# A transformer layer on one core: heads visited three score tiles at a time, sums in groups of 384 and 128 queries, and stacks loaded 16 rows at a time

## The chip, the cores and the metric

The kernel runs on one core of a Trainium2 chip. The metric is the device time of one execution in microseconds (us). PE is TensorE, DVE is VectorE, ACT is ScalarE, POOL is GpSimd and SP is SyncE, which here only issues DMAs and waits.

## The reference

One layer on 4 sequences of 2048 tokens, width 256: layer norm, then attention with 16 heads of 16 channels and a learned bias by relative position, plus a feed-forward branch scaled by a router's gate, plus the residual. The change is in the attention:

```python
    q, k, v = (qkv[:, :, 0], qkv[:, :, 1], qkv[:, :, 2])
    scores = jnp.einsum('bhqd,bhkd->bhqk', q, k)
    scores = scores + compute_bias(rel_emb, S, S)
    attn = jax.nn.softmax(scores.astype(jnp.float32), axis=-1).astype(scores.dtype)
    out = jnp.einsum('bhqk,bhkd->bhqd', attn, v)
    out = jnp.transpose(out, (0, 2, 1, 3)).reshape(B, S, EMBED_DIM)
    return out @ W_out
```

The bias varies only where key and query are near each other; further off it has one constant value on each side.

## The kernel before

**Two stages.** The first (one block of code, up to 584 us) computes layer norm, the feed-forward branch, q, k and v, and stores q and k in DRAM (`qk_d`), each as a high and a low part. It also takes the row maxima of the scores of the first two heads ("early" maxima). The second stage is the attention, 64 heads (4 sequences by 16) one after the other, then the output projection.

**Tiles of a head.** The scores are computed transposed: a score tile is 128 keys (key block `kb`, 16 of them) by 512 queries (chunk `c`, four of them), so 64 tiles a head. For each, the kernel runs:

- PE, `scores` (L1039): one matmul of 49 rows by 512 columns into one of three PSUM banks in turn (`RING = 3`); the 49th row subtracts the query's maximum. It waits on `drained` until the tile that had the bank before has been read.
- ACT, L899: the exponential, from the bank to the buffer `prob`, which holds `PROBS = 3` key blocks of 2048 queries.
- POOL, L946: multiplies the few queries near the key block by the exponential of their bias (`near_parts`).
- PE, `sums` (L1048): four matmuls per key block, one for each chunk of 512 queries, each 32 columns of values (`vx`, or `vr` on the other side of the diagonal) by 512 queries, in plain 32-bit. The four go to the four 32-partition groups of bank 7, and each is two records in the trace. The sums of a key block come two key blocks after its scores (`LAG = 2`).

**Maxima of a later head.** Behind every score matmul PE runs one of `maxima` (L1029) for the head two further on (`LEAD = 2`): 48 rows by 512 columns, on the other half of the array's rows, into banks 3 to 6. DVE takes the maximum over two banks at once (L980: 128x1 out of 128x1024), two such reductions per key block. Banks 3 and 4 are written again once their reduction is done, and so are 5 and 6. At the end of a head DVE combines the maxima, transposes them (L987, L993) and SP writes them as the 49th row of `q_st` (`shift`, four DMAs).

**Order.** Each engine's program is written out by hand, in order. PE's, for one key block: score 0, maxima 0, score 1, maxima 1, score 2, maxima 2, score 3, maxima 3, then the sums of the key block two back. For the last two heads there are no maxima left, and scores use seven banks (from `ALONE` on).

**Loads.** `load(n)` on SP brings head n's q and k into `q_st` and `k_st` with four DMAs. Two of them have 32 rows with an outer dimension of two (two copies of a part, or two parts), two have 16 rows; each row is 8 KB. `near`, the bias factors, is one DMA per head. At the stage's start SP's order is `load(0)`, the rows of ones (four DMAs), `shift(0)`, then `load(1)` and `load(2)`. PE's first score waits for head 0, the ones and `shift(0)`, and, since the maxima of head 2 run beside it, for `load(2)` too (L1068 to L1073).

**Normalising.** When a head's sums are done ACT copies bank 7 to `o_sb`, SP spreads the totals over partitions, DVE takes reciprocals (L999), SP spreads these, POOL multiplies, and SP keeps the result in `attn` with four DMAs. All of that runs beside the next head.

Of the kernel before, what the change touches and what calls it, by code (L numbers as in the profile page):

```python
# [14 lines left out]
H, D = 16, 16  # L15
# [28 lines left out]
PROBS = 3  # L44
# [30 lines left out]
def near_parts(kb):  # L75

    first = P * kb - NEAR
    c = first // CH
    at, end = first - CH * c, min(first + NQ, S)
    if first < 0:  # L80
        return [(0, end, 0, PAD - first)]
    if at == PAD:
        return [(first - PAD, end, 0, 0)]
    if at + NQ + PAD == CH:
        return [(first, first + NT, 1, 0)]
    left = [(first, min(CH * (c + 1), end), 1, 0)]
    return left + ([(CH * (c + 1), end, 0, PAD + CH - at)] if end > CH * (c + 1) else [])


def left_chunks(kb):  # L90

    first = P * kb - NEAR
    return 0 if first < 0 else first // CH + (first % CH != PAD)


NEAR_UP_TO = [sum(len(near_parts(i)) for i in range(kb)) for kb in range(KB + 1)]


def near_at(kb, c):

    found = [i for i, part in enumerate(near_parts(kb)) if part[0] // CH == c]
    return NEAR_UP_TO[kb] + found[0] + 1 if found else 0


def sum_order(kb):

    return sorted(range(CPB), key=lambda c: (near_at(kb, c) > 0, c))
# [25 lines left out]
def transformer_layer(nc, x, w_qkv, w_out, rel_emb, router_w, w1, b1, w2, b2, hot, out):  # L133
# [7 lines left out]
    def load_stacks(sp, n, q_stack, k_stack, loaded):  # L141

        for which, stack, loads in ((0, q_stack, Q_LOADS), (1, k_stack, K_LOADS)):
            for row, part, parts, copies in loads:
                rows = qk_d[which, part:part + parts, bass.ds(D * n, D), :]
                if copies > 1:
                    rows = rows.to_broadcast([copies, D, S])
                sp.dma_start(stack[D * row:D * (row + parts * copies), :].bitcast(F32), rows).then_inc(loaded, 16)  # L148
# [6 lines left out]
    with ctx:  # L155
# [12 lines left out]
        max_half = sb("max_half", [P, 2, KB, 2])  # L168
# [537 lines left out]
        with c2:  # L706
# [6 lines left out]
            prob = sb("prob", [P, PROBS, S], c=c2)  # L713
# [53 lines left out]
            PIECE = 16  # L767

            TOTAL_AT, NORM_AT = 6, 10

            def tile_at(n, kb, c):

                return CPB * (KB * n + kb) + c

            ALONE = tile_at(NH - LEAD, 0, 0)
# [9 lines left out]
            def summed(n, kb, c):  # L785

                return CPB * (KB * n + kb) + sum_order(kb).index(c) + 1
# [4 lines left out]
            def _(sp):  # L792
                def load(n):
# [4 lines left out]
                    wait(sp, near_done, NEAR_UP_TO[KB] * (n - GROUP + 1))  # L798
# [28 lines left out]
                def keep(n):  # L827
# [17 lines left out]
                load(0)  # L845
                sp.wait_ge(ones_set, 1)
                for u in range(GROUP):
                    sp.dma_start(k_st[u][ROWS:ROWS + 1, :].bitcast(F32), ones_row).then_inc(ones_in, 16)  # L848
                shift(0)
                for n in range(1, GROUP - 1):  # L850
                    load(n)
                for n in range(NH):
                    if n + GROUP - 1 < NH:
                        load(n + GROUP - 1)
                    if n + 1 < NH:
                        shift(n + 1)
# [23 lines left out]
            def _(act):  # L880
                def collect(n):

                    act.wait_ge(pv_done, CPB * KB * (n + 1))

                    if n > 1:
                        act.wait_ge(attn_in[(n - 2) // H], 16 * CPB * ((n - 2) % H + 1))
                    nc.scalar.activation(o_sb[:, n % 2], ps[:, SUM_BANK], ACT.Copy).then_inc(o_copied, 1)  # L887

                def head(n):
                    for kb in range(KB):  # L890
                        if kb == LAG and n > 0:
# [228 lines left out]
```

## Time and profile before

| | us |
|---|---|
| median of 3 runs | 3373.62 (3371.6 to 3377.18) |
| the profiled execution | 3374.15 |
| its span | 3372.3 |

Outside the span lie 1.85 us. Busy time in the span: PE 3177.7 us (94%), DVE 2757.9 (82%), ACT 2407.5 (71%), POOL 1284.7 (38%). Overlapping matmuls count once, and a matmul's record covers its way through the array, so PE's 94% is not a statement of how fully it is used. A line such as L980 is a line of the kernel above. "Idle before" is the time in which an engine stood still just ahead of an instruction, and the name behind the arrow is what it waited for.

### The profile page before, as it was taken

The numbers are of one execution on the slowest core, as the hardware profiler recorded it, in microseconds if no ns is written. First come the engines' busy times: TensorE is split into PE (matmuls) and PEld (weight loads), VectorE is DVE, ScalarE is ACT, GpSimd is POOL, SyncE is SP. The second block draws the span as 40 slices with busy tenths as digits, with TensorE's granted clock in tenths as the row PEclk, the third lists the DMA queues.
The fourth block names the chain that finished last, engine by engine and source line by source line (L and its number), as shares of the span: only waits on it lengthen the run. The fifth ranks groups of instructions, "written<-read, shape, count | busy, mean of one in ns | idle before, by whom it ended". The sixth has DMA issues, their size and how long they took to land.

```text
span 3372.3 us, 56315 instructions
## 1 busy us (share of the span) xinstructions
PE 3177.7 (94%) x19978; PEld 1549.5 (46%) x19978; DVE 2757.9 (82%) x3078; ACT 2407.5 (71%) x4667; POOL 1284.7 (38%) x1662
## 2 busy tenths in 40 slices
PE   8899999499999999999999999999999999999998
PEld 6788888133333333333333333333333333333336
DVE  5477765399999999999999999999999999999932
ACT  4344344388887788887788887788887788888784
POOL 1112112244444444444444444444444444444445
PEclk9999999699999999999999999999999999999999
DMA  7332232121111111111111111111111111111005
GB/s 188 101 100 82 76 111 84 55 63 35 35 35 35 35 35 35 35 35 35 35 36 35 35 36 36 35 37 37 36 35 35 36 35 36 35 35 35 26 10 180
DMA packets 124515, 174.40 MB, mean 52 GB/s; under 512 B 44952, under 2 KB 84568, under 8 KB 117896
## 3 DMA queue, kind: packets, MB, share of 16 engines
q1 hardware_dynamic: 124232, 170.80, 18.5%
q8 instruction: 157, 2.57, 0.3%
q14 instruction: 126, 1.03, 0.1%
HBM read 110.31 MB, written 56.69 MB: 50 GB/s over the span
## 4 chain that ended last, share of the span: by engine, by line
PE 59%; ACT 18%; issue 3%; DMA 2%; SPq 1%; DVE 0%; POOL 0%; ACTq 0%; DVEq 0%
PE ps L1060 30%; PE ps L1045 28%; ACT prob L899 18%; DMA k_st<-qk_parts 1%; PE ps L1093 1%; DMA out_rows<-base_in 1%; PE ps L1034 0%; SPq L148 0%; DVE max_half L980 0%; DMA base_in<-base_rows 0%; SPq L848 0%; SPq L806 0%; POOL turned L954 0%; ACT o_sb L887 0%; DMA recip_rows<-recip_all 0%
## 5 line engine op out<-in xcount | busy, mean ns | idle before, releaser
L980 DVE TENSOR_REDUCE max_half<-ps 128x1 f32<-128x1024 f32 x1984 | 2337.3, 1220 | 280.2 <-PE ps L1034 264.8
L899 ACT ACTIVATE prob<-ps 128x512 f32<-128x512 f32 x4096 | 2115.3, 603 | 555.6 <-PE ps L1045 554.4
L1045 PE MATMUL ps<-q_st,k_st 49*128 49x512 f32 x4096 | 1487.4, 444 | 153.2 <-DMA k_st<-qk_parts 49.0
L1034 PE MATMUL ps<-k_st,q_st 48*128 48x512 f32 x3968 | 1573.8, 470 | 0.3 <-DVE max_half L980 0.2
L946 POOL TENSOR_TENSOR prob<-prob,near 128x224 f32<-128x224 f32 (+2 forms) x1408 | 965.3, 692 | 1559.0 <-ACT prob L899 1536.3
L1045 PEld LDWEIGHTS ps<-q_st,k_st 49*128 49x128 f32 x4096 | 679.8, 185 | 1372.2 <-ACT prob L899 1217.1
L1060 PE MATMUL ps<-prob,vx 128*32 128x512 f32 x4096 | 948.6, 607 | 0.0
L1060 PE MATMUL ps<-prob,vr 128*32 128x512 f32 x4096 | 947.5, 605 | 0.0
L1034 PEld LDWEIGHTS ps<-k_st,q_st 48*128 48x128 f32 x3968 | 656.5, 184 | 71.7 <-DVE max_half L980 2.9
L616 PE MATMUL ps<-xnt,w_parts 128*128 128x512 f32 x1152 | 277.3, 400 | 16.9 <-DMA k_early<-qk_parts 10.6
L616 PEld LDWEIGHTS ps<-xnt,w_parts 128*128 128x128 f32 x1152 | 218.5, 191 | 70.5 <-DMA k_early<-qk_parts 10.8
L557 ACT ACTIVATE parts<-ps 128x512 fp32r<-128x512 f32 x64 | 38.3, 599 | 273.2 <-PE ps L616 233.7
L1060 PEld LDWEIGHTS ps<-prob,vr 128*32 128x32 f32 x4096 | 133.2, 108 | 176.2 <-ACT prob L899 153.5
L681 PE MATMUL ps<-w_parts,hid 128*128 128x256 f32 x1536 | 196.3, 284 | 0.0
L681 PEld LDWEIGHTS ps<-w_parts,hid 128*128 128x128 f32 x1536 | 183.9, 189 | 11.7 <-issue 11.7
L1060 PEld LDWEIGHTS ps<-prob,vx 128*32 128x32 f32 x4096 | 132.6, 108 | 80.2 <-ACT prob L899 54.9
L368 POOL TENSOR_TENSOR top_exp<-euler,top_less 128x32 f32<-128x32 f32 x16 | 86.8, 5427 | 160.7 <-DVE top_less L421 160.7
L362 POOL TENSOR_TENSOR rstd<-var_eps,power 128x4 f32<-128x4 f32 x17 | 23.1, 1358 | 308.5 <-DVE var_eps L396 308.5
L565 ACT ACTIVATE hid_raw<-ps,b_sb 128x512 f32<-128x512 f32 x128 | 88.3, 690 | 42.2 <-PE ps L616 32.4
L466 DVE TENSOR_TENSOR parts<-ps,parts 128x512 fp32r<-128x512 f32 x64 | 44.3, 692 | 72.5 <-ACT parts L557 72.4
L483 DVE TENSOR_TENSOR hid<-hid_raw,hid 128x512 fp32r<-128x512 f32 x128 | 85.5, 690 | 19.3 <-ACT hid L572 17.9
L456 DVE TENSOR_REDUCE max_early<-ps 128x2 f32<-128x1024 f32 x64 | 78.4, 1225 | 19.2 <-PE ps L625 18.9
(66 smaller groups left out, 931.0 us busy)
## 6 DMA issues: line engine op xcount, KB each, us to landing
qk_parts<-parts SPq DMA_DIRECT2D x64, 512.0 KB, 4.7
near<-bias_near SPq DMA_DIRECT2D x64, 352.0 KB, 13.5
q_st<-qk_parts SPq DMA_DIRECT2D x64, 256.0 KB
k_st<-qk_parts SPq DMA_DIRECT2D x64, 256.0 KB
x_sb<-in_L_attn_hidden_states SPq DMA_DIRECT2D x18, 512.0 KB, 6.2
base_rows<-x_sb SPq DMA_DIRECT2D x16, 512.0 KB, 2.9
q_st<-qk_parts SPq DMA_DIRECT2D x64, 128.0 KB
k_st<-qk_parts SPq DMA_DIRECT2D x64, 128.0 KB
```

The lines of the kernel that those rows point to most:

```text
L368: nc.gpsimd.tensor_tensor(top_exp[:], euler[:], top_less[:], ALU.pow).then_inc(exp_done, 1)
L456: nc.vector.tensor_reduce(max_early[:, :, bass.ds(i, 1), j], ps[:, 0:2].unsqueeze(2), AX.X, ALU.max).then_inc(max_done, 1)
L483: nc.vector.tensor_tensor(hid[:, 1, f], hid_raw[:, f % RAWS], hid[:, 0, f].bitcast(F32), ALU.subtract).then_inc(hid_low, 1)
L565: nc.scalar.activation(hid_raw[:, f % RAWS], ps[:, F1_BANKS[f % 4]], ACT.Gelu_apprx_tanh, bias=b1_sb[:, f:f + 1]) \
L616: last = nc.tensor.matmul(to, stationary(a, k), moving(b, k), start=k == 0 and (a, b) == PASSES[0], stop=k == blocks - 1 and (a, b) == PAS ...
L681: last = nc.tensor.matmul(ps[:, F2_BANKS[t % 2], E * (t // 2):E * (t // 2 + 1)], hid[:, a, f, P * t:P * (t + 1)], weight(W_2, b_, f), star ...
L899: nc.scalar.activation(prob[:, t % PROBS, CH * c:CH * (c + 1)], ps[:, bank_of(tile_at(n, kb, c))], ACT.Exp) \
L946: nc.gpsimd.tensor_tensor(at, at, near[n % GROUP][:, side, c0:c0 + q1 - q0], ALU.mult).then_inc(near_done, 1)
L980: nc.vector.reduce_max(max_half[:, m % 2, i, half:half + 1], ps[:, MAX_BANK + 2 * half:MAX_BANK + 2 + 2 * half].rearrange("p a n -> p (a n ...
L1034: mm = nc.tensor.matmul(ps[:, MAX_BANK + c], query_block(q_st[u][0:ROWS], i), k_st[u][0:ROWS, CH * c:CH * (c + 1)], start=True, stop=True)
L1045: nc.tensor.matmul(ps[:, bank_of(at)], k_st[u][:, P * kb:P * (kb + 1)], q_st[u][:, CH * c:CH * (c + 1)], start=True, stop=True).then_inc(s ...
L1060: nc.tensor.matmul(ps[32 * c:32 * (c + 1), SUM_BANK], v[:, n % 2, kb], prob[:, (KB * n + kb) % PROBS, CH * c:CH * (c + 1)], start=kb == 0, ...
```

## The change

A head is no longer 16 visits of four tiles but 22 **visits**: for each block of three key blocks, three visits of one key block and queries 0 to 1535 (three tiles), then one visit of the last 512 queries of all three key blocks (three tiles); the 16th key block gives one visit of three tiles and one of a single tile. `prob` holds `PROBS = 4` visits of 1536 columns. The lag of two now counts visits.

- **Sums.** A visit of one key block has four matmuls of 384 queries. A visit of the last queries has four matmuls of 128 queries for each of its key blocks, so twelve. Each visit's sums wait for all its tiles, and ACT waits for a whole visit's sums before it writes the buffer again.
- **Maxima.** Three tiles in a visit are one reduction over two banks and one over a single bank; the single tile is one over one bank. `max_groups` gives each reduction the banks that came free longest ago. Each maxima matmul waits for its own bank.
- **Loads.** `load(n)` is six DMAs of 16 rows. SP's order at the stage's start becomes `load(0)`, `load(2)`, `shift(0)`, the ones, `near` of head 0, `load(1)`, then `near` of 1 and 2.
- **Keep** is eight DMAs a head, since the groups are split at query 1536. The points in a head at which POOL builds values and normalises, and DVE takes reciprocals, are restated in visits (11, 15, 9).

```diff
-PROBS = 3
+PROBS = 4
-Q_LOADS = [(0, 0, 1, 2), (2, 1, 1, 1)]
-K_LOADS = [(0, 0, 2, 1), (2, 0, 1, 1)]
-STACK_LOADS = len(Q_LOADS) + len(K_LOADS)
+Q_PARTS = [0, 0, 1]
+K_PARTS = [0, 1, 0]
+STACK_LOADS = len(Q_PARTS) + len(K_PARTS)
...
+def head_visits():
+
+    visits = []
+    for kb in range(0, KB, WIDE):
+        block = range(kb, min(kb + WIDE, KB))
+        visits += [[(k, c) for c in range(WIDE)] for k in block]
+        visits.append([(k, WIDE) for k in block])
+    return visits
...
+def max_groups():
+
+    freed = {bank: bank - CPB for bank in range(CPB)}
+    groups, order = [], {}
+    for m in range(LEAD, NH):
+        k = 0
+        for v, visit in enumerate(VISITS):
+            for size in ([2, 1] if len(visit) == WIDE else [1] * len(visit)):
+                at = len(groups)
+                choices = [range(bank, bank + size) for bank in range(CPB + 1 - size)]
+                banks = min(choices, key=lambda taken: sorted((freed[bank] for bank in taken), reverse=True))
+                tiles = sorted(range(size), key=lambda i: freed[banks[i]])
+                for j, i in enumerate(tiles):
+                    order[m, k + j] = at, k + i, banks[i], freed[banks[i]], j == size - 1
+                for bank in banks:
+                    freed[bank] = at
+                groups.append((m, k, banks))
+                k += size
+    return groups, order
...
             def _(pe):
-                def maxima(m, i, c):
-
-                    if c % 2 == 0:
-                        wait(pe, max_done, 2 * (KB * m + i) + c // 2 - 1)
+                def maxima(m, at):
+
+                    _, k, bank, before, last = MAX_ORDER[m, at]
+                    wait(pe, max_done, EARLY + before + 1 if before >= 0 else 0)
...
+                    pe.wait_ge(drained, tile_at(n, *visit[-1]) + 1)
+                    if NEAR_UP_TO[v + 1] > NEAR_UP_TO[v]:
+                        pe.wait_ge(near_done, NEAR_UP_TO[NV] * n + NEAR_UP_TO[v + 1])
+                    buffer = prob[:, (NV * n + v) % PROBS]
+                    if visit[0][1] == 0:
+                        kb = visit[0][0]
+                        for g, side in enumerate(near_parts(kb, MAIN_GROUPS)[1]):
+                            nc.tensor.matmul(ps[32 * g:32 * (g + 1), SUM_BANK, 0:MAIN], (vr if side else vx)[:, n % 2, kb],
+                                             buffer[:, MAIN * g:MAIN * (g + 1)], start=kb == 0, stop=False).then_inc(pv_done, 1)
+                    else:
+                        for j, (kb, _) in enumerate(visit):
+                            for g, side in enumerate(near_parts(kb, TAIL_GROUPS)[1]):
+                                mm = nc.tensor.matmul(ps[32 * g:32 * (g + 1), SUM_BANK, MAIN:CH], (vr if side else vx)[:, n % 2, kb],
+                                                      buffer[:, CH * j + TAIL * g:CH * j + TAIL * (g + 1)], start=False, stop=kb == KB - 1)
```

The order of PE's program in the middle of the stage, before, is that of one key block (scores on L1045, maxima on L1034, sums on L1060; the number behind `q_st` and `k_st` is the pair of heads that share the tensor):

```order
L1045 MATMUL ps<-q_st0,k_st0 128x512 [waits drained]
L1034 MATMUL ps<-k_st0,q_st0 128x512 [waits max_done]
L1045 MATMUL ps<-q_st0,k_st0 128x512 [waits drained]
L1034 MATMUL ps<-k_st0,q_st0 128x512
L1045 MATMUL ps<-q_st0,k_st0 128x512 [waits drained]
L1034 MATMUL ps<-k_st0,q_st0 128x512 [waits max_done]
L1045 MATMUL ps<-q_st0,k_st0 128x512 [waits drained]
L1034 MATMUL ps<-k_st0,q_st0 128x512
L1060 MATMUL ps<-prob,vr 32x512 [waits drained] x3
L1060 MATMUL ps<-prob,vx 32x512 [waits near_done]
```

Of the changed kernel, the same engine, one visit that is followed by the twelve short sums of a visit of last queries (scores on L1108, maxima on L1097, short sums on L1130):

```order
L1108 MATMUL ps<-q_st1,k_st1 128x512 [waits drained]
L1097 MATMUL ps<-k_st1,q_st1 128x512 [waits max_done]
L1108 MATMUL ps<-q_st1,k_st1 128x512 [waits drained]
L1097 MATMUL ps<-k_st1,q_st1 128x512 [waits max_done]
L1108 MATMUL ps<-q_st1,k_st1 128x512 [waits drained]
L1097 MATMUL ps<-k_st1,q_st1 128x512 [waits max_done]
L1130 MATMUL ps<-prob,vx 32x128 [waits near_done,drained]
L1130 MATMUL ps<-prob,vx 32x128 x11
L1108 MATMUL ps<-q_st1,k_st1 128x512 [waits drained]
```

The fourth score has left the visit, every maxima matmul has a wait of its own, and a run of twelve short matmuls stands where four long ones stood (in the other visits four of 32x384).

The order of SP's DMAs at the stage's start, before:

```order
L148 DMA q_st<-qk_parts 32x1x2048
L148 DMA q_st<-qk_parts 16x2048
L148 DMA k_st<-qk_parts 32x1x2048
L148 DMA k_st<-qk_parts 16x2048
L799 DMA near<-bias_near 128x704
L848 DMA k_st<-base_in 1x16x128 [waits ones_set]
L848 DMA k_st<-base_in 1x16x128 x3
L806 DMA q_st<-neg_turn 1x16x32 [waits neg_turned]
L806 DMA q_st<-neg_turn 1x16x32 x3
L148 DMA q_st<-qk_parts 32x1x2048
L148 DMA q_st<-qk_parts 16x2048
L148 DMA k_st<-qk_parts 32x1x2048
```

And of the changed kernel:

```order
L194 DMA q_st<-qk_parts 16x2048 x3
L194 DMA k_st<-qk_parts 16x2048 x3
L194 DMA q_st<-qk_parts 16x2048 x3
L194 DMA k_st<-qk_parts 16x2048 x3
L860 DMA q_st<-neg_turn 1x16x32 [waits neg_turned]
L860 DMA q_st<-neg_turn 1x16x32 x3
L906 DMA k_st<-base_in 1x16x128 [waits ones_set]
L906 DMA k_st<-base_in 1x16x128 x3
L853 DMA near<-bias_near 128x704
L194 DMA q_st<-qk_parts 16x2048 x3
L194 DMA k_st<-qk_parts 16x2048 x3
```

Head 2's stacks have moved from the third place to the second, `near` of head 0 behind the ones, and no load has an outer dimension of two any more.

## Rows read from the trace of the kernel before

**Rows 1.** The page: one group of its costliest instructions; busy, mean ns; idle before.

```profile
L980 DVE TENSOR_REDUCE max_half<-ps 128x1 f32<-128x1024 f32 x1984 | 2337.3, 1220 | 280.2 <-PE ps L1034 264.8
```

**Rows 2.** The chain that ended last, one key block: start us, us, what.

```profile
2010.62 0.44 PE ps L1045
...
2011.08 0.61 ACT prob L899
2011.68 0.04 issue
2011.73 0.50 PE ps L1045
```

**Rows 3.** Waits, 1000 to 3200 us: in total, times, longest.

```profile
PEld ps L1045 <- ACT prob L899: 1012.8, 1626, 0.8
```

**Rows 4.** Timeline of PE, one key block: start us, us, instruction.

```profile
2006.94 0.62 PE L1060 MATMUL ps<-prob,vr 128*32 128x512 f32 x1
2006.95 0.62 PE L1060 MATMUL ps<-prob,vx 128*32 128x512 f32 x1
...
2007.40 0.59 PE L1060 MATMUL ps<-prob,vr 128*32 128x512 f32 x1
...
2007.94 0.50 PE L1045 MATMUL ps<-q_st,k_st 49*128 49x512 f32 x1
...
2008.28 0.39 PE L1045 MATMUL ps<-q_st,k_st 49*128 49x512 f32 x1
...
2008.51 0.39 PE L1045 MATMUL ps<-q_st,k_st 49*128 49x512 f32 x1
...
2009.12 0.49 PE L1045 MATMUL ps<-q_st,k_st 49*128 49x512 f32 x1
...
2009.55 0.62 PE L1060 MATMUL ps<-prob,vr 128*32 128x512 f32 x2
```

**Rows 5.** Groups by line and shape, 1000 to 3200 us, costliest first.

```profile
L1045 PE MATMUL ps<-q_st,k_st 49*128 49x512 f32 x3357 | 1222.9, 444 | 88.2 <-ACT prob L899 24.6
...
L946 POOL TENSOR_TENSOR prob<-prob,near 128x224 f32<-128x224 f32 x420 | 279.7, 666 | 325.1 <-ACT prob L899 309.8
...
L999 DVE RECIPROCAL recip<-total_sb 128x16 f32<-128x16 f32 x52 | 12.6, 243 | 0.0
```

**Rows 6.** Timeline of DVE and of ACT, the same stretch; idle time and releaser bracketed.

```profile
2008.74 2.36 DVE L980 TENSOR_REDUCE max_half<-ps 128x1 f32<-128x1024 f32 x2 [0.25 <-PE ps L1034]
...
2008.47 2.07 ACT L899 ACTIVATE prob<-ps 128x512 f32<-128x512 f32 x4 [0.55 <-PE ps L1045]
```

**Rows 7.** Timeline of all engines where the attention stage begins.

```profile
574.79 9.23 PE L681 MATMUL ps<-w_parts,hid 128*128 128x256 f32 x77
...
578.41 0.43 DVE L500 TENSOR_TENSOR ffn_sb<-ps,b_sb 128x256 f32<-128x256 f32 x1 [2.40 <-PE ps L681]
...
588.58 1.09 SPq L148 DMA_DIRECT2D q_st<-qk_parts  x2
...
591.45 2.49 SPq L848 DMA_DIRECT2D k_st<-base_in  x4
593.99 2.48 SPq L806 DMA_DIRECT2D q_st<-neg_turn  x4
...
607.26 1.04 POOL L930 TENSOR_TENSOR vr<-vx,near 128x512 f32<-128x512 f32 x1 [15.52 <-DMA near<-bias_near]
...
633.02 0.76 PE L1045 MATMUL ps<-q_st,k_st 49*128 49x512 f32 x1 [49.00 <-DMA k_st<-qk_parts]
```

**Rows 8.** DMA, 595 to 633 us: GB/s in 40 equal slices.

```profile
GB/s 55 63 54 164 17 147 115 269 52 172 17 42 55 43 26 52 205 222 130 52 52 52 52 172 69 104 38 61 52 52 67 307 88 54 54 54 54 52 52 47
```

**Rows 9.** DMA issues by line over the whole span: count, KB, us to landing.

```profile
q_st<-neg_turn SPq DMA_DIRECT2D x256, 2.0 KB, 2.2
```

**Rows 10.** Stretches: us, busy by engine, PE clock, DMA share, GB/s.

```profile
645.00:675.00 30.00, 29.00 (x176) 10.88 (x168) 24.83 (x22) 21.47 (x43) 11.28 (x17) 0.91 0.00 1
...
3270.00:3306.00 36.00, 36.00 (x212) 14.00 (x213) 0.25 (x1) 35.38 (x71) 17.23 (x24) 1.00 0.04 9
```

More of the change, by code:

```diff
@@ L90, in left_chunks @@
[L90 to L107, printed above, removed]
+WIDE = 3
+QUEUE = WIDE * CH
+MAIN = QUEUE // CPB
+TAIL = (S - QUEUE) // CPB
@@ new lines @@
+MAIN_GROUPS = [(MAIN * g, MAIN * (g + 1)) for g in range(CPB)]
+TAIL_GROUPS = [(QUEUE + TAIL * g, QUEUE + TAIL * (g + 1)) for g in range(CPB)]
+def head_visits():
[5 more added lines that the diff above has]
+    return visits
+VISITS = head_visits()
+NV = len(VISITS)
+TILE = {tile: i for i, tile in enumerate(tile for visit in VISITS for tile in visit)}
@@ new lines, in near_parts @@
+def near_parts(kb, groups):
+    first, last = P * kb - NEAR, P * kb - NEAR + NQ
+    parts, sides = [], []
+    for q0, q1 in groups:
+        if q1 <= first or q0 >= last:
+            sides.append(1 if q1 <= first else 0)
+            continue
+        if q0 < first and q1 > last and first - q0 == PAD:
+            side, at, end = 0, q0, last
+        else:
+            side = 1 if q0 < first or (q1 <= last and parts and parts[-1][2] == 1) else 0
+            at, end = max(q0, first, 0), min(q1, last)
+            assert not (q0 < first and q1 > last) or q1 - last == PAD
+            end = q1 if q0 < first and q1 > last else end
+        if parts and parts[-1][1] == at and parts[-1][2] == side:
+            parts[-1][1] = end
+        else:
+            parts.append([at, end, side])
+        sides.append(side)
+    return [(at, end, side, at - first + (0 if side else PAD)) for at, end, side in parts], sides
@@ new lines, in visit_parts @@
+def visit_parts(visit):
+    parts = []
+    for j, (kb, c) in enumerate(visit):
+        if c == WIDE:
+            parts += [(kb, c, CH * j - QUEUE, part) for part in near_parts(kb, TAIL_GROUPS)[0]]
+    if visit[0][1] == 0:
+        parts = [(visit[0][0], (part[1] - 1) // CH, 0, part) for part in near_parts(visit[0][0], MAIN_GROUPS)[0]]
+    return parts
+NEAR_UP_TO = [sum(len(visit_parts(visit)) for visit in VISITS[:v]) for v in range(NV + 1)]
+def max_groups():
[16 more added lines that the diff above has]
+    return groups, order
@@ L110, in bucket_line @@
+MAX_GROUPS, MAX_ORDER = max_groups()
 def bucket_line():
@@ L141, in load_stacks @@
     def load_stacks(sp, n, q_stack, k_stack, loaded):
[L143 to L148, printed above, removed]
+        for which, stack, used in ((0, q_stack, Q_PARTS), (1, k_stack, K_PARTS)):
+            for row, part in enumerate(used):
+                sp.dma_start(stack[D * row:D * (row + 1), :].bitcast(F32), qk_d[which, part, D * n:D * (n + 1), :]).then_inc(loaded, 16)
     def query_block(stack, i):
@@ L845, in _ @@
                 load(0)
+                load(LEAD)
+                shift(0)
                 sp.wait_ge(ones_set, 1)
@@ L1063, in _ @@
                 for n in range(NH):
                     m = n + LEAD
-                    for kb in range(KB):
-                        if kb == 0:
+                    for v, visit in enumerate(VISITS):
+                        if v == 0:
                             pe.wait_ge(shift_in[n % GROUP], 16 * SHIFT_LOADS * (n // GROUP + 1))
```

147 lines of the change are left out of this document (72 added, 75 removed).

## The prediction

> **What bounds the kernel now.** I read the page first. Only DVE's maxima (L980) come near PE in busy time, and their idle time is put down to PE [rows 1]. Busy shares can't settle it, so I read the chain of waits in the middle of the stage. The reader should see a loop: the first score of a key block 0.44 us, its exponential 0.61, 0.04 to PE, the fourth score 0.50, which needs the bank that this exponential gives back [rows 2]. Then come the sums, and the next key block starts behind them. By the waits, 1012.8 us of 2200 are weight loads of scores that stand for ACT, 1626 times [rows 3]. So the bound is not an engine but three banks for four tiles. A key block takes 2011.73 - 2009.12 = 2.61 us [rows 2, 4], and 3357 scores in 2200 us give 64 x 2200 / 3357 = 41.94 us a head [rows 5], that is 16 x 2.61 and 0.2 more.
>
> Next I ask who is late next. In one key block [rows 4]: first pair (score and maxima run side by side) to second 2008.28 - 2007.94 = 0.34; to a third that waits for nothing 0.23; a pair that had to wait to the sums 0.43; the first half of the sums 0.46; the second half to the next pair 0.54. A pair that waits costs 0.11 more (0.34 against 0.23), its weights. ACT does four exponentials in 2.07, 0.49 apart [rows 6]. DVE does two reductions in 2.36, a record being 1.22 [rows 1, 6], so 1.14 apart; its gap is 0.25 a key block. DVE has 9% to spare, PE more, ACT most.
>
> **The stage's start.** PE stands 49.00 us, to 633.02, for a DMA into `k_st` [rows 7]. SP had begun at 588.58. The throughput shows why: over long stretches it lies at 52 to 54 GB/s, where other slices reach 307 [rows 8], so few of the sixteen DMA engines work. The DMAs with an outer dimension of two, two of each head's four, are the likely cause, and head 2 is the third head in that queue. The changed loads all have 16 rows outermost, as the other two have now. The Trainium skill ("DMA: Bandwidth & Descriptors", why a DMA increments its semaphore by 16) says that the outermost dimension caps how many engines share a DMA, two here and sixteen after; the plateau agrees. With the queue gone, what is left is SP's issuing: 0.55 us a load (1.09 for two), 0.62 for each of the ones and the shift (2.49 and 2.48 for four) [rows 7]. Twelve loads, four shifts, four ones: 588.58 + 12 x 0.55 + 8 x 0.62 = 600.1, and 2.2 to land, as the shift's DMAs take [rows 9], with some for the queue: PE starts at 602.7, **30.3 us** earlier. Two things cut that. `near` of head 0 now goes out at 600.2; before it went behind four loads, so near 591, and had landed at 607.26 [rows 7], 16 us, beside the slow loads. Spread traffic should make it 4 to 8 (an estimate), in time for the first sums, due three visits on at about 608; at the old 16 us plus 1.04 for `vr` they wait till 617, a loss of 9. And the clock: the granted clock is 0.91 in 645 to 675 [rows 10], so at half (1.2 GHz) for the first 5.4 of these, 17.4 us of work at the low level since 633.02. A visit is then bound by PE at nearly twice 1.67 (below), 3.2 instead of 1.9: 17.4 / 3.2 = 5.4 visits at 1.3 more, 7 us. Before, some 4 were lost to the same thing (an estimate: ACT, which keeps its pace, has a part in its loop). Net gain of the start: 30.3 - 3 = **27 us**, bounds 18 and 31.
>
> **A visit of three tiles.** The three banks now fit: tile 0 of a visit needs the exponential of the tile 0 before it, 0.44 + 0.61 + 0.04 = 1.09 after its score, which is before PE is back. The ring loop is gone. What remains:
>
> - PE: pairs 0.34 + 0.23, last pair to sums 0.43 - 0.11 = 0.32, sums of 384 queries a quarter of 0.43 less per half, 0.35 + 0.43. Sum **1.67**.
> - ACT: 3 x 0.49 = **1.47**; its waits on sums are one a visit instead of four.
> - DVE: a two-bank reduction 1.14; a one-bank one isn't in the trace. Two rows bound it: 0.43 for 256 elements [rows 7] and 1.22 for 1024 [rows 1], so 0.69 for 512 on the line between them, and 0.61 apart (below it can't be under 0.43, above not over 1.14). Sum **1.75** a visit. Per head 21 x 1.75 + 0.61 + 0.24 for the reciprocals [rows 5] and as much again for each of the two small steps at a head's end, at most, = **38.0 us**.
> - The maxima's banks, a new loop. The order of banks repeats every three visits: in two of three the second matmul of the pair needs the bank of the previous two-bank reduction, in the third both do. The loop: reduction 1.22, 0.04 to PE, a matmul with its weights 0.50, 0.07 to DVE (2008.28 + 0.39 against 2008.74) [rows 2, 4, 6] = 1.83; where both wait, 0.34 + 0.39 instead of 0.50: 2.06. Mean (2 x 1.83 + 2.06) / 3 = **1.91**.
>
> The last is the longest, so 21 x 1.91 = 40.1, plus the single tile's reduction 0.61 and the small DVE work 0.6 to 0.7 at the head's turn, plus some 0.2 for the copy of bank 7: **41.6 us a head against 41.94**. DVE moves into PE's place, and the freed ring gives almost nothing. At 0.3 us a head, 62 heads: **-19 us**, bounds 40.5 (-89) and 42.3 (+22), since 0.05 in this loop is 1 us a head.
>
> **Visits of last queries.** Twelve matmuls of 128 queries, 24 records instead of 8, in six rounds of four side by side. A long round is 0.43 (0.46 with the first weights), nearly all streaming; a quarter of it is 0.11. Six rounds and the ends are 0.81 against 0.78: nothing, if the cost goes with the columns. PE's slack against 1.91 is 0.24 a visit, which would cover 0.04 a round. Above, the bound is the slowest rate the trace shows for records this short: 77 matmuls of 256 columns in 9.23 us, 0.12 each [rows 7]; 24 x 0.12 = 2.9 us. I take the low end, since within one round the matmuls start 0.01 us apart (2006.94, 2006.95 [rows 4]), so that one has no such price of its own.
>
> Rule against it: the Trainium skill ("TensorE: Matmul & The Clock Gate", back-to-back issue gap) says that with hardware decode off about 62 ns go per MATMUL however short. No row here shows which mode this is. By it the short sums would be 24 x 0.062 = 1.5 us, an estimate by that page, and the kernel slower (rival 1 has the mechanism, priced from rows).
>
> **The rest.** POOL has five multiplications in the visit of last queries of key blocks 12 to 14, three of 224 queries at 0.67 [rows 5] and two of 96, which take less: 2.0 to 3.3 us. They have from the first exponential's end, 1.09, to the sums behind the next visit and the single tile, 2 x 1.91 + 0.43 = 4.25, so 3.2: hidden, or 0.1 a head (6 us) at worst. Keep's four more DMAs are 2.5 us of SP, which waits most of a head. SP's `shift` stands behind two more loads (1.1 us), due a head later: nothing. PE's whole-visit wait on tiles two visits old: nothing. The last two heads are ACT's (35.38 busy of 36) [rows 10]: 128 tiles at 0.53 now, perhaps 0.50 with fewer waits, -3, bounds 0 and -5. First stage and projection are untouched.
>
> **Sum**, against the profiled execution (3374.15, within 0.02% of the median): 3374.15 - 27 - 19 - 3 = **3325**.
>
> **Rivals.**
>
> 1. *Short matmuls have a price each, slower.* PE is within 0.24 us a visit of the loop. If the 24 cost more than 0.81 + 0.24, each of the 5.3 such visits in a head lengthens it. The start's gain of 30 allows 0.5 us a head and the forecast's 0.3 more, 0.8 / 5.3 = 0.15 a visit; so it decides from 1.2 us, 0.05 a record. At half the row's 0.12: 24 x 0.06 = 1.44, +0.39 x 5.3 = 2.1 a head: 3325 + 130 = 3455. At 0.12: 1.85 x 5.3 = 9.8, 3933. For: each has its weight load, and nothing this short is in the trace of the stage. Against: the 0.01 between starts, though a queue filled during a wait could hide a price there.
> 2. *DVE reaches its floor.* If PE answers sooner, the head goes towards 38.0. At 40.0: 3325 - 62 x 1.6 = 3226; at 40.8: 3275. For: PE's queue holds the matmul ready. Against: 0.50 and 0.07 are latencies of the rows, not waits.
> 3. *Only the start gains.* Small slips in the loop (POOL, the copy of bank 7, PE and DVE 0.2 apart and waiting for each other in turn) make the head 41.9 to 42.5: 3343 to 3380.
> 4. *The start gains less*: `near` comes late and costs 9 (or the narrow queue was not the cause and all 27 are gone: 3352). Its chance, 0.1, lies across the others and inside the range.
>
> **How the numbers follow.** Forecast, head 41.1 to 41.9, 3293 to 3343: 0.40. Rival 3: 0.20, a quarter of it within 0.2% (about what a measurement can tell from no change, 3367 to 3380). Rival 2, 3220 to 3293: 0.15. Rival 1, 3380 up: 0.25. Faster 0.40 + 0.15 + 0.15 = 0.70, same 0.05, slower 0.25. The range leaves out the lower half of rival 2 (0.07) and the upper half of rival 1 (0.13): 3265 to 3440.
>
> **What would show it.** PE's first score near 603; throughput without the plateau at 53. In the middle: DVE busy over 90% with gaps of about 0.1 and 0.3 by turns, PE's maxima (L1097) waiting for DVE, ACT no longer the releaser of scores; a one-bank reduction near 0.69; short sums 0.11 from round to round. Rival 1 shows as rounds of 0.2 and more on L1130, with DVE waiting for PE in one visit of four. The forecast is wrong if a head is not within 41.1 to 41.9, or PE starts after 610.

## The result, and the profile after

The changed kernel takes **3269.66 us** (median of four, 3268.9 to 3271.32) against 3374.09, a ratio of 0.9691, 95% interval 0.9674 to 0.9708. The forecast was 3325, with a range of 3265 to 3440: the direction held, and the gain, 104 us, is twice the 49 that the sum gave. The time lies inside the range, at its lower end.

The page of the changed kernel: span, busy time by engine, the chain that ended last, and the groups that answer to [rows 1] and to the sums.

```profile
span 3267.8 us, 72368 instructions
...
PE 3200.7 (98%) x28170; PEld 1717.4 (53%) x28170; DVE 2813.3 (86%) x3760; ACT 2439.0 (75%) x4667; POOL 1297.9 (40%) x1918
...
PE 77%; DVE 3%; DMA 2%; issue 1%; SPq 0%; POOL 0%; ACT 0%; DVEq 0%; ACTq 0%
...
L1042 DVE TENSOR_REDUCE max_half<-ps 128x1 f32<-128x512 f32 (+1 forms) x2666 | 2398.1, 945 | 121.5 <-PE ps L1097 118.1
...
L1097 PE MATMUL ps<-k_st,q_st 48*128 48x512 f32 x3968 | 1403.2, 450 | 8.5 <-DVE max_half L1042 7.1
...
L1130 PE MATMUL ps<-prob,vx 128*32 128x128 f32 x7040 | 276.0, 277 | 0.5 <-POOL prob L1007 0.4
```

The chain was 59% PE and 18% ACT; now ACT has left it and DVE has come in with 3%. Where the 104.4 us of span went is read from the first score of each head (64 scores a head), from SP's first load of the stage and from the last score:

| part | forecast | measured |
|---|---|---|
| first stage, to SP's first stack load (588.58, now 577.74) | 0 | -10.8 |
| from there to PE's first score (44.4, now 16.5) | -30.3 | -27.9 |
| head 0 (46.0, now 43.3) | +3 | -2.7 |
| heads 1 to 61 | -19 | -71.5 |
| heads 62 and 63 (33.8 and 32.5, now 36.8 and 35.4) | -3 | +5.9 |
| from the last score to the end | 0 | +2.6 |
| sum | -49 | -104.4 |

**The start.** Timeline of the changed kernel where the attention stage begins (start us, us, engine, instruction; idle time and releaser in brackets); it answers to [rows 7]:

```profile
577.74 1.27 SPq L194 DMA_DIRECT2D q_st<-qk_parts  x3
...
583.21 2.49 SPq L860 DMA_DIRECT2D q_st<-neg_turn  x4
585.74 2.48 SPq L906 DMA_DIRECT2D k_st<-base_in  x4
...
594.27 0.76 PE L1108 MATMUL ps<-q_st,k_st 49*128 49x512 f32 x1 [21.08 <-DMA k_st<-base_in]
...
594.43 1.04 POOL L991 TENSOR_TENSOR vr<-vx,near 128x512 f32<-128x512 f32 x1 [13.54 <-DMA near<-bias_near]
```

PE is released by the ones at 594.27, 16.5 us after SP began, and `near` of head 0 has landed in time. SP issues a load in 0.45 us, less than the 0.55 taken, so the last of the ones goes out 10.5 us after SP's first load; it lands 6 us later, not the 2.2 of [rows 9]. The throughput has no plateau any more. In 577 to 594 us the DMA share in tenths (40 slices) is 9 in over half of the slices, and the queue's packets take 94.3% of the time of sixteen engines. Between 595 and 633 us of the kernel before they took 27.9%. So the engines are shared out now, and they are nearly full:

```profile
DMA  0000994949779399393996949389399399989997
GB/s 0 0 0 0 308 309 77 231 58 212 77 77 193 39 116 193 39 231 39 154 154 77 193 58 251 39 96 174 39 116 156 28 122 112 86 146 358 401 154 154
...
q1 hardware_dynamic: 832, 2.24, 94.3%
```

**The middle.** Groups by line and shape, 1000 to 2900 us of the changed kernel (busy us, mean ns, idle before by releaser), and two lines of its waits, these of 1000 to 3000 us (total, times, longest):

```profile
L1042 DVE TENSOR_REDUCE max_half<-ps 128x2 f32<-128x1024 f32 x979 | 1195.9, 1222 | 77.6 <-PE ps L1097 75.1
...
L1042 DVE TENSOR_REDUCE max_half<-ps 128x1 f32<-128x512 f32 x1026 | 694.0, 680 | 0.0
```

```profile
PEld ps L1097 <- DVE max_half L1042: 80.8, 352, 0.6
...
DVE max_half L1042 <- PE ps L1097: 78.7, 344, 0.5
```

2984 scores in these 1900 us give 40.75 us a head, against 41.94 [rows 5]. DVE is busy 1820.8 of the 1900 us, 96%. The one-bank reduction, which the trace before did not have, takes 680 ns (forecast 0.69). From its start to the next start it is 0.598 where nothing holds DVE up; for a two-bank reduction that is 1.141.

One visit of the changed kernel, PE's matmuls (scores L1108, maxima L1097, sums L1125), then the reductions of the same stretch:

```profile
2004.81 0.52 PE L1125 MATMUL ps<-prob,vr 128*32 128x384 f32 x2
...
2005.16 0.49 PE L1125 MATMUL ps<-prob,vr 128*32 128x384 f32 x2
...
2005.59 0.50 PE L1108 MATMUL ps<-q_st,k_st 49*128 49x512 f32 x1
2005.60 0.50 PE L1097 MATMUL ps<-k_st,q_st 48*128 48x512 f32 x1
2005.93 0.39 PE L1108 MATMUL ps<-q_st,k_st 49*128 49x512 f32 x1
2005.97 0.49 PE L1097 MATMUL ps<-k_st,q_st 48*128 48x512 f32 x1
2006.17 0.39 PE L1108 MATMUL ps<-q_st,k_st 49*128 49x512 f32 x1
2006.31 0.39 PE L1097 MATMUL ps<-k_st,q_st 48*128 48x512 f32 x1
2006.63 0.52 PE L1125 MATMUL ps<-prob,vr 128*32 128x384 f32 x3
```

```profile
2004.69 1.23 DVE L1042 TENSOR_REDUCE max_half<-ps 128x2 f32<-128x1024 f32 x1 [0.23 <-PE ps L1097]
...
2005.83 0.68 DVE L1042 TENSOR_REDUCE max_half<-ps 128x1 f32<-128x512 f32 x1
...
2006.50 1.22 DVE L1042 TENSOR_REDUCE max_half<-ps 128x2 f32<-128x1024 f32 x1
```

DVE starts the two-bank reduction at 2004.69 and is done at about 2005.91. The second maxima matmul of the visit, which needs that bank, starts 0.05 to 0.06 later, at 2005.97; it takes 0.49, and 0.04 behind it the next two-bank reduction starts, at 2006.50. From 2004.69 that is 1.81. From one visit's start of the sums to the next, 2004.81 to 2006.63, it is 1.82. Between 1000 and 2900 us there are 978 stretches from one two-bank reduction to the next. 526 of them last 1.81 or 1.82 and 278 last 2.04 to 2.06, the two lengths of the loop of the maxima's banks (forecast 1.83 and 2.06). The others lie at a head's turn (111) and beside the reciprocals in the middle of a head (64).

**The short sums**, 24 records of 128 columns, and the pair behind them:

```profile
2000.94 0.86 PE L1130 MATMUL ps<-prob,vx 128*32 128x128 f32 x24
2001.73 0.49 PE L1108 MATMUL ps<-q_st,k_st 49*128 49x512 f32 x1
```

They take 0.79 from first start to the next pair, where the eight records of 384 columns take 0.78 (2004.81 to 2005.59): 0.033 us a record. The price by columns was right. The Trainium skill ("TensorE: Matmul & The Clock Gate", back-to-back issue gap) names 62 ns for each MATMUL with hardware decode off, which would be 1.5 us for the 24, an estimate by that page. The trace shows 0.79, about half of that. So that price isn't paid here; which mode the runs had no row shows.

### The profile page after: what moved, and what is told of

Same layout as the page of the kernel before. It is cut to its first block, busy times and chain, and to the rows that moved or that the text cites. A ratio compares the mean times of both kernels' runs of the same rounds, so it can differ in the third digit from the quotient of the medians.

```text
span 3267.8 us, 72368 instructions
## 1 busy us (share of the span) xinstructions
PE 3200.7 (98%) x28170; PEld 1717.4 (53%) x28170; DVE 2813.3 (86%) x3760; ACT 2439.0 (75%) x4667; POOL 1297.9 (40%) x1918
## 4 chain that ended last, share of the span: by engine, by line
PE 77%; DVE 3%; DMA 2%; issue 1%; SPq 0%; POOL 0%; ACT 0%; DVEq 0%; ACTq 0%
PE ps L1108 27%; PE ps L1125 24%; PE ps L1097 18%; PE ps L1130 8%; DVE max_half L1042 2%; DMA out_rows<-base_in 1%; PE ps L1165 0%; DMA k_st<-base_in 0%; DMA base_in<-base_rows 0%; SPq L194 0%; POOL prob L1007 0%; DVE neg_turn L1055 0%; SPq L860 0%; POOL turned L1015 0%; ACT turned L967 0%
## 5 line engine op out<-in xcount | busy, mean ns | idle before, releaser
L1042 DVE TENSOR_REDUCE max_half<-ps 128x1 f32<-128x512 f32 (+1 forms) x2666 | 2398.1, 945 | 121.5 <-PE ps L1097 118.1
L960 ACT ACTIVATE prob<-ps 128x512 f32<-128x512 f32 x4096 | 2156.3, 600 | 440.4 <-PE ps L1108 428.4
L1108 PE MATMUL ps<-q_st,k_st 49*128 49x512 f32 x4096 | 1407.3, 442 | 21.4 <-DMA k_st<-base_in 21.1
L1097 PE MATMUL ps<-k_st,q_st 48*128 48x512 f32 x3968 | 1403.2, 450 | 8.5 <-DVE max_half L1042 7.1
L1108 PEld LDWEIGHTS ps<-q_st,k_st 49*128 49x128 f32 x4096 | 658.8, 184 | 747.3 <-ACT prob L960 681.1
L1125 PE MATMUL ps<-prob,vr 128*32 128x384 f32 x4864 | 756.3, 498 | 0.0
L1097 PEld LDWEIGHTS ps<-k_st,q_st 48*128 48x128 f32 x3968 | 636.9, 184 | 180.7 <-DVE max_half L1042 103.3
L1125 PE MATMUL ps<-prob,vx 128*32 128x384 f32 x3328 | 593.5, 499 | 1.1 <-issue 1.1
L1125 PEld LDWEIGHTS ps<-prob,vr 128*32 128x32 f32 x4864 | 133.4, 108 | 325.5 <-issue 221.4
L1130 PE MATMUL ps<-prob,vx 128*32 128x128 f32 x7040 | 276.0, 277 | 0.5 <-POOL prob L1007 0.4
L1130 PEld LDWEIGHTS ps<-prob,vx 128*32 128x32 f32 x7040 | 190.3, 109 | 109.5 <-issue 63.8
L1125 PEld LDWEIGHTS ps<-prob,vx 128*32 128x32 f32 x3328 | 103.2, 108 | 48.5 <-issue 40.2
L529 DVE TENSOR_TENSOR hid<-hid_raw,hid 128x512 fp32r<-128x512 f32 x128 | 85.4, 688 | 18.8 <-ACT hid L618 17.4
```

What stands on the lines that cost most here:

```text
L529: nc.vector.tensor_tensor(hid[:, 1, f], hid_raw[:, f % RAWS], hid[:, 0, f].bitcast(F32), ALU.subtract).then_inc(hid_low, 1)
L960: nc.scalar.activation(prob[:, t % PROBS, CH * j:CH * (j + 1)], ps[:, bank_of(at)], ACT.Exp).then_inc(drained, 1)
L1042: nc.vector.tensor_reduce(max_half[:, m % 2].rearrange("p i c -> p (i c)")[:, k:k + len(banks)], tiles, AX.X, ALU.max) \
L1097: mm = nc.tensor.matmul(ps[:, MAX_BANK + bank], query_block(q_st[u][0:ROWS], k // CPB), k_st[u][0:ROWS, CH * (k % CPB):CH * (k % CPB + 1)] ...
L1108: nc.tensor.matmul(ps[:, bank_of(at)], k_st[u][:, P * kb:P * (kb + 1)], q_st[u][:, CH * c:CH * (c + 1)], start=True, stop=True).then_inc(s ...
L1125: nc.tensor.matmul(ps[32 * g:32 * (g + 1), SUM_BANK, 0:MAIN], (vr if side else vx)[:, n % 2, kb], buffer[:, MAIN * g:MAIN * (g + 1)], star ...
```

## The experiments

Each changes the kernel named and is read from its own trace. "Heads" is the mean of heads 1 to 61 in us, counted by their scores, as above. `e1_loads`, `e4_visits`, `e8_singles` and `e11_alternate` were executed four times, the others once; four executions of the kernel before lie within 0.17% of each other, or 6 us.

**The loads, taken apart.** `e1_loads` is the kernel before with both edits to the loads: 16 rows, and the new order at the stage's start.

```diff
-        for which, stack, loads in ((0, q_stack, Q_LOADS), (1, k_stack, K_LOADS)):
+        for which, stack, used in ((0, q_stack, Q_PARTS), (1, k_stack, K_PARTS)):
+            for row, part in enumerate(used):
+                sp.dma_start(stack[D * row:D * (row + 1), :].bitcast(F32), qk_d[which, part, D * n:D * (n + 1), :]).then_inc(loaded, 16)
...
                 load(0)
+                load(LEAD)
+                shift(0)
                 sp.wait_ge(ones_set, 1)
```

> The kernel before, with the changed loads alone: six DMAs of 16 rows a head, and the new order at the stage's start. Theory: the two gaps of PE for a DMA into the key stacks are what the loads are worth. In the first stage PE stood 10.6 us for k_early; that goes. The attention stage then starts 16.5 us after SP does, as in the changed kernel, instead of 44.4. Sum 10.8 + 27.9 = 38.7: 3374 - 38.7 = 3335, heads unchanged at 41.94. Rival: part of the earlier start is given back at the first sums, since near of head 0 goes out later; then 3341 to 3345.

Measured: 3330.85 us against 3373.55, ratio 0.9873 (0.9856 to 0.9889), so -42.7. Heads stay 41.95. SP starts the stage 12.5 us earlier than before, and PE starts 16.3 us after SP's first load instead of 44.4.

`e2_rows16` has the 16 rows and the old order:

```diff
-Q_LOADS = [(0, 0, 1, 2), (2, 1, 1, 1)]
-K_LOADS = [(0, 0, 2, 1), (2, 0, 1, 1)]
+Q_PARTS = [0, 0, 1]
+K_PARTS = [0, 1, 0]
```

> The kernel before with DMAs of 16 rows, in the old order at the stage's start. Theory: the width of the DMAs is the whole cause and the order nearly nothing, since SP issues three loads in 18 x 0.45 = 8 us: PE starts the stage 17 to 18 us after SP, against 44.4 before, and the gap of 10.6 in the first stage is gone. 3336 to 3338. Rival: the order matters as much as the width; then the stage starts 25 to 30 us after SP, 3345 to 3350.

Measured: 3340.73. PE starts 24.1 after SP, so at this width the order is worth 7.8 us there, more than I had expected. Half of that is SP's issuing: the last load that PE waits for has gone out 14.4 us after SP's first, where in `e1_loads` the last of the ones has gone out after 10.5. The other half is a longer time to land, 9.7 us instead of 5.8. A likely reason, not shown by itself, is that head 1's stacks and two `near` stand ahead in the queue while the sixteen engines are nearly full (94% of their time there).

`e3_order` has the new order and the old shapes:

```diff
                 load(0)
+                load(LEAD)
+                shift(0)
                 sp.wait_ge(ones_set, 1)
...
-                shift(0)
                 for n in range(1, GROUP - 1):
-                    load(n)
+                    load_near(n)
```

> The kernel before with the new order at the stage's start alone, loads with an outer dimension of two as before. Theory: a narrow load holds two DMA engines some 10 to 15 us, and two of them instead of three stand before PE's start, so 44.4 becomes about 30, and the gap of 10.6 in the first stage stays: 3374 - 14 = 3360. If the width were not the cause, 3336 to 3340.

Measured: 3361.13, -12.4. PE starts 31.1 after SP (44.4 before), and SP itself starts as late as before, at 587.77. So the width is worth 20.3 us at the stage's start in the old order (44.4 to 24.1), the order 13.3 at the old width and 7.8 at the new. Only the runs with 16 rows start the stage 10.8 to 13.5 us earlier.

That earlier start is a second place where the narrow loads were waited for, in the first stage. Timeline of PE, before and then after:

```profile
149.76 0.52 PE L681 MATMUL ps<-w_parts,hid 128*128 128x256 f32 x3
160.88 5.16 PE L616 MATMUL ps<-xnt,w_parts 128*128 128x512 f32 x12 [10.60 <-DMA k_early<-qk_parts]
```

```profile
149.77 2.64 PE L727 MATMUL ps<-w_parts,hid 128*128 128x256 f32 x21
152.24 2.96 PE L662 MATMUL ps<-xnt,w_parts 128*128 128x512 f32 x12
```

`load_stacks` also fills `q_early` and `k_early` for the early maxima. PE stood 10.60 us for them in the kernel before and doesn't stand at all now. From there on the changed kernel is 10.8 us ahead (155.13 instead of 165.97 for the first early maxima), and it still is when the attention stage begins.

**The visits alone.** `e4_visits` is the changed kernel with loads and order as before.

```diff
-Q_PARTS = [0, 0, 1]
-K_PARTS = [0, 1, 0]
+Q_LOADS = [(0, 0, 1, 2), (2, 1, 1, 1)]
+K_LOADS = [(0, 0, 2, 1), (2, 0, 1, 1)]
```

> The changed kernel with the loads and their order as before: visits, groups and banks alone. Theory: heads of 40.77 instead of 41.94, so 3270 + 38.7 = 3308 and the parts add up. Rival: the narrow loads also slow the changed kernel inside the stage (near and the stacks late for the shorter heads); then over 3315, heads over 41.

Measured: 3313.44 against 3373.55, ratio 0.9822 (0.9807 to 0.9836), -60.1, and heads of 40.80. With the 42.7 of the loads that is 102.8, so the two parts add up to the whole 104 within what these runs tell apart. Inside the stage, past its start, the narrow loads cost nothing that shows (40.80 against 40.77).

**Was the ring the bound before?** `e9_before_singles` is the kernel before with a reduction over one bank for every tile, so that DVE has less to do and no maxima matmul has to wait for it.

```diff
-                    for half in range(2):
-                        dve.wait_ge(max_ready, 2 * (KB * m + i) + half + 1)
+                    for c in range(CPB):
+                        dve.wait_ge(max_ready, EARLY + CPB * (KB * (m - LEAD) + i) + c + 1)
...
-                                             ps[:, MAX_BANK + 2 * half:MAX_BANK + 2 + 2 * half].rearrange("p a n -> p (a n)"), AX.X).then_inc(max_done, 1)
+                        nc.vector.reduce_max(max_half[:, m % 2, i, c:c + 1], ps[:, MAX_BANK + c], AX.X).then_inc(max_done, 1)
```

> The kernel before, four tiles a visit, with a reduction over one bank for every tile. DVE then needs 64 x 0.60 + 0.6 = 38.9 us a head, and no maxima matmul waits for it. Theory: the kernel before is bound by the ring of three score banks alone, so heads stay 41.9, 3370 to 3376. Rival: part of the 41.94 is the exchange of banks with DVE, as in the changed kernel; then heads fall under 41.5, below 3345.

Measured: 3367.98 against 3372.56, heads 41.93. The 5 us are not in these heads; most of them are in head 0, 42.7 us instead of 46.0. What makes the changed kernel much faster (below) is worth nothing on top of the ring of three banks for four tiles. The first step of the prediction stands.

**Loop of banks, or throughput of DVE?** Four versions of the changed kernel. `e5_single_short` shortens the one-bank reduction to 256 of its 512 columns; the maxima of the rest are left out.

```diff
+                    if len(banks) == 1:
+                        tiles = tiles[:, :, 0:CH // 2]
                     nc.vector.tensor_reduce(max_half[:, m % 2].rearrange("p i c -> p (i c)")[:, k:k + len(banks)], tiles, AX.X, ALU.max) \
```

> The changed kernel, whose reductions over one bank read 256 of the 512 columns (maxima of the other half are left out). Theory, the loop of the maxima's banks: what sets a visit is the two-bank reduction, the matmul into a bank it frees, and the next two-bank reduction, 1.81 or 2.05; the one-bank reduction lies inside it. So shortening it by 0.27 changes nothing: heads 40.6 to 40.8, 3262 to 3270. Rival, DVE's throughput: DVE is busy 96%, 22 x 0.27 = 5.9 less a head, down to PE's 1.67 a visit: heads about 36.5 to 37, 3010 to 3030.

Measured: 3266.18, heads 40.74. The two groups of reductions, 1000 to 2900 us:

```profile
L1044 DVE TENSOR_REDUCE max_half<-ps 128x2 f32<-128x1024 f32 x980 | 1200.4, 1225 | 336.5 <-PE ps L1099 328.8
...
L1044 DVE TENSOR_REDUCE max_half<-ps 128x1 f32<-128x256 f32 x1026 | 421.4, 414 | 0.0
```

The one-bank reduction is 414 ns instead of 680, so DVE saves 273 us, and nearly all of that turns up as idle time before the two-bank reduction: 336.5 instead of 77.6. DVE's throughput was not the bound, although it was busy 96% of the time.

`e6_pair_short` shortens the two-bank reduction to 384 of each 512 columns; the rest is left out.

```diff
+                    if len(banks) == 2:
+                        tiles = tiles[:, :, 0:3 * CH // 4]
                     nc.vector.tensor_reduce(max_half[:, m % 2].rearrange("p i c -> p (i c)")[:, k:k + len(banks)], tiles, AX.X, ALU.max) \
```

> The changed kernel, whose reductions over two banks read 384 of each 512 columns (the rest is left out). The two-bank reduction is 0.27 shorter. Theory, the loop: 1.81 and 2.05 become 1.54 and 1.78, so two visits of three fall to PE's own 1.67 and the third to 1.78: mean 1.71, heads 21 x 1.71 + 1.2 = 37.1, 3270 - 61 x 3.7 = 3045. Rival, PE: if PE with 1.81 a visit is the bound by itself (its chain is 77% PE), nothing changes: 3265 to 3270.

Measured: 3089.16, heads 37.92. The same 0.27 us off the other reduction gives 2.8 us a head. The forecast was 37.1; the mean of the 21 visits is 1.74, not 1.71, and the single tile's visit takes 1.35, not 1.2. That PE was the bound at 1.81 is out as well.

`e7_fixed_pairs` lets every two-bank reduction wait for the one before, by giving it the same banks always.

```diff
-                choices = [range(bank, bank + size) for bank in range(CPB + 1 - size)]
+                choices = [range(0, 2)] if size == 2 else [range(2, 3), range(3, 4)]
```

> The changed kernel, whose two-bank reductions always take banks 3 and 4 and the one-bank reductions 5 and 6 in turn. Both matmuls of every pair then wait for the reduction before, as now in one visit of three. Theory, the loop: every visit 2.05, heads 21 x 2.05 + 1.2 = 44.3, 3270 + 61 x 3.5 = 3484. Rival, DVE's throughput: DVE's work is the same, so heads stay 40.8: 3270.

Measured: 3465.62, heads 43.91. Of 908 stretches from one two-bank reduction to the next, 858 last 2.04 to 2.06. The work of each engine is that of the changed kernel; the choice of banks alone costs 196 us.

`e8_singles` goes the other way: one-bank reductions only, so that every maxima matmul waits for the fourth reduction back.

```diff
-            for size in ([2, 1] if len(visit) == WIDE else [1] * len(visit)):
+            for size in [1] * len(visit):
```

> The changed kernel with a reduction over one bank for every tile, four banks in turn. Each matmul waits for the reduction four back, so there is no loop left; DVE's throughput is the bound. A one-bank reduction has a record of 0.68 and 0.61 to 0.65 apart: 3 x 0.61 = 1.83 a visit, 64 x 0.61 + 0.7 = 39.7 a head, 3270 - 61 x 1.1 = 3203. If they are 0.65 apart, 42.3 a head, 3363. Rival, PE is the bound at 1.81 a visit: 3270.

Measured: **3139.14 us** against 3370.69, ratio 0.931 (0.9295 to 0.9326), heads 38.73. Its reductions, 1000 to 2900 us:

```profile
L1042 DVE TENSOR_REDUCE max_half<-ps 128x1 f32<-128x512 f32 x3142 | 1885.6, 673 | 0.3
```

DVE has 64 reductions a head instead of 43. By their spacing that is 64 x 0.598 = 38.3 us of work instead of 21 x (1.141 + 0.598) + 0.598 = 37.1, and the kernel is still faster. DVE has no idle time at all, 0.3 us of 1900, and with 0.45 for the rest of a head the sum is 38.7, as measured. I had taken 0.61. Here DVE's throughput is the bound; in the changed kernel it wasn't.

**Two mixtures.** `e10_mixed` uses three one-bank reductions only where a two-bank one would have to take both banks of its predecessor.

```diff
+            sizes = [2, 1] if len(visit) == WIDE else [1] * len(visit)
+            best = min((max(freed[b], freed[b + 1]), min(freed[b], freed[b + 1])) for b in range(CPB - 1))
+            if sizes[0] == 2 and best[0] == best[1]:
+                sizes = [1] * WIDE
+            for size in sizes:
```

> The changed kernel; a visit whose two-bank reduction would take both banks of the reduction before gets three reductions over one bank instead (10 of 21 visits, no visit of 2.05 is left). Theory, the loop: a visit with a two-bank reduction behind another 1.81, one of single reductions 1.80, so heads 21 x 1.81 + 1.2 = 39.2 and 3270 - 61 x 1.6 = 3172. Rival: what made the version with single reductions fast is only that DVE never waits; here it waits in some visits, but the mean falls between 38.7 and 40.8 anyway, so the sharp test is 39.2 against less than 38.7.

Measured: 3149.52, heads 38.83. The rule picks 6 of 21 visits, not the 10 that I wrote, and the result is better than 39.2. The 1.81 binds only where a two-bank reduction stands behind another and needs its bank, two visits of four here; of the other two one takes 1.68 and one mostly 1.84, so that the mean is 1.79. I had counted 1.81 for every visit.

`e11_alternate` has a two-bank reduction in every other visit.

```diff
-            for size in ([2, 1] if len(visit) == WIDE else [1] * len(visit)):
+            for size in ([2, 1] if len(visit) == WIDE and v % 2 == 0 else [1] * len(visit)):
```

> The changed kernel with a two-bank reduction in every other visit only, one-bank reductions for all other tiles. No two-bank reduction follows another closely, so there is no loop; DVE's throughput is the bound: 11 x 1.141 + 42 x 0.598 + 0.5 = 38.2 a head against 38.73 with single reductions, 3139 - 61 x 0.55 = 3106. Rival: a matmul that waits for the two-bank reduction still makes DVE wait once in two visits; then 38.7 to 39.5, 3139 to 3185.

Measured: **3124.29 us** against 3372.56, ratio 0.9264 (0.9248 to 0.9279), heads 38.46 (forecast 38.2). Waits, 1000 to 2900 us:

```profile
DVE max_half L1042 <- PE ps L1097: 15.8, 49, 0.6
...
PEld ps L1097 <- DVE max_half L1042: 8.7, 43, 0.2
```

15.8 us of DVE waiting are left where the changed kernel had 75. This is the fastest version of the study, 145 us under the changed kernel by one line.

A version in which a two-bank reduction takes any two banks, neighbours or not, was not tried.

## Why the prediction came out as it did

The gain exceeds the sum by 55 us. The step that failed most is one term of the sum, "41.6 us a head": it measured 40.77, which is 52 us over 61 heads. The second is the first stage, put at nothing, which gave 10.8. Head 0 gave 5.7 more than forecast. The last two heads, the start and the end took 8.9, 2.4 and 2.6 the other way.

- **What bounds the kernel before: right.** It is the ring, not DVE, and not the exchange with DVE (`e9_before_singles`).
- **The stage's start: right in cause, off in its terms.** Narrow DMAs are the cause, 20.3 us by themselves. I priced what is left as SP's issuing and 2.2 us to land, 14.1, and it is 16.5: 10.5 of issuing and 6.0 to land. That the ones land late because the sixteen engines are nearly full is likely, but not tested by itself. The rival that `near` comes late did not happen.
- **"First stage and projection are untouched": wrong.** I followed the changed loader only to the stage in which the diff shows it called. It is called in the first stage too, and there PE's 10.60 us stood in the trace of before. 10.8 us.
- **The clock: wrong size.** I took 17.4 us at the low level over from the trace before. The granted clock of the changed kernel, by stretch:

```profile
584.00:604.00 20.00, 9.18 (x36) 4.33 (x40) 6.25 (x7) 5.99 (x12) 3.64 (x5) 0.50 1.05 160
604.00:650.00 46.00, 45.69 (x446) 21.25 (x442) 43.90 (x52) 38.11 (x74) 18.65 (x31) 1.00 0.27 41
```

It is 0.50 (1.2 GHz) to 604 and 1.00 (2.4 GHz) from there, so only some 10 us of work ran at the low level; PE had stood 21 us before it instead of 49. Head 0 is 2.7 faster where I had added 3. Two other traces show that the shorter standstill is not why the clock rose sooner. `e1_loads` has the old pattern of work behind a standstill of 20.8 us, `e4_visits` the new one behind 49.5 us; from the first score to the rise:

```profile
592.40:609.40 17.00, 16.80 (x64) 6.59 (x64) 11.78 (x10) 10.57 (x20) 5.64 (x8) 0.50 0.82 138
...
634.80:645.20 10.40, 9.84 (x40) 4.29 (x40) 6.93 (x8) 6.32 (x12) 2.60 (x4) 0.50 0.13 53
```

The pattern of work doesn't settle it alone either: `e9_before_singles` rises after 10.2 us and `e10_mixed`, with visits, after 16.5. What sets it stays open. The price was too high as well: in `e10_mixed` head 0 is 5.2 us longer than the later heads, where I had 7 for 17.4 us at the low level.

- **The loop of the maxima's banks: right, and the term that was mis-sized.** It is the bound, with 1.81 and 2.05 for my 1.83 and 2.06, as `e5_single_short`, `e6_pair_short` and `e7_fixed_pairs` show. The mean of the 21 visits is 1.88, not 1.91: the 0.07 from matmul to DVE is 0.04 here, and a visit at the head's turn takes 1.69. That is 0.6 us a head. For the single tile and the head's turn I had added 1.5, and that visit takes 1.22: 0.3 more. Together 0.85 us in 41.6, two per cent, and times 61 heads 52 us, more than the whole forecast gain. My bounds for the term (40.5 to 42.3) held the measured 40.77.
- **Short sums: right.** 0.79 and 0.78. Rival 1 is out.
- **Rival 2** gave 3226 to 3275 if PE answers sooner and DVE comes near its floor of 38.0 us a head. The measured time lies just inside. PE and DVE do answer each other some 0.02 sooner than I had it, a small part of this rival; but DVE still waits 75 us in 1900, and less work for it gained nothing (`e5_single_short`).
- **The last two heads: wrong.** I took them for ACT's by 35.38 busy of 36 [rows 10]. The chain of the kernel before in such a head, and of the changed one, start us, us, what:

```profile
3281.42 1.00 PE ps L1060 x8
3282.42 1.11 PE ps L1045 x4
```

```profile
3151.28 0.78 PE ps L1125 x8
3152.06 0.89 PE ps L1108 x3
...
3158.29 2.62 POOL prob L1007 x5
```

It is PE in both, 1.00 + 1.11 for four tiles before, 0.78 + 0.89 for three now: 0.53 and 0.56 a tile. A quarter less of each takes 0.22 off, so 0.12 of the sums and 0.22 to 0.23 of the scores go with the visit and not with its size. These 0.34 are paid 22 times instead of 16: 2.0 of the 3.0 us that such a head is longer. (The 1.67 is the figure that the sum had for PE.) POOL's five multiplications, 2.62 us, which I had found nearly hidden at 1.91 a visit, do show at 1.67: the single tile's visit takes 1.46 instead of 1.21, some 0.25 a head. The rest isn't split further. Overlapped records had made ACT look full. Together +5.9 instead of -3.
- **The end, +2.6**, is not explained. From the last score to the end it is 66.3 to 68.0 in the five kernels without the visits and 68.1 to 70.6 in the eight with them, so about 2 us go with the visits, and the rest differs from run to run.

## What to carry to other kernels

Busy share says little where engines hand banks to each other: with DVE at 96%, the same work in smaller pieces, 64 reductions a head instead of 43, was 130 us faster, and 273 us less work changed nothing. Follow each circle of "bank free, refill, start again" and compare its length with the time between two uses, and try another choice of banks or of piece sizes before another layout. For every helper that a diff changes, look up all its callers and their waits in the trace; and an error of two per cent in a loop that makes up nine tenths of the time is as large as most gains, so quote its bounds in the sum.

## What the runs showed of the hardware

- Where DMAs whose outermost dimension is two are what is left in the queue, the throughput lies at 52 to 54 GB/s [rows 8]. With 16 rows there is no such level and the mean is 132 GB/s (577 to 594 us): the same 768 KB a head, and PE's start 20 us sooner (`e2_rows16`). That agrees with the Trainium skill ("DMA: Bandwidth & Descriptors", why a DMA increments its semaphore by 16), which lets the outermost dimension set the number of engines.
- 48 records (24 weight loads and 24 matmuls of 128 columns, plain 32-bit, in four column groups) go through PE in 0.79 us, with the next pair's start included.
- Reductions out of PSUM on DVE start 0.598 us apart for 512 columns and 1.141 for 1024. So a two-bank reduction saves only 0.055 us over two one-bank ones, and here holds two banks for 1.22 us instead of 0.68.
- How long TensorE's clock stays at its low level at the start of the attention stage doesn't follow the standstill ahead of it: 17.2 us after 49.0 and 17.0 after 20.8 with the old pattern of work, 10.4 after 49.5 and 9.7 after 21.1 with the new one (16.5 in `e10_mixed`).
